# A fused attention and expert kernel: the first step's four gate and up pieces are also stored split, and loaded finished seven steps later

## What is computed

```python
gate = jnp.einsum('btd,edf->ebtf', x, Wg)
up = jnp.einsum('btd,edf->ebtf', x, Wu)
gate = gate.at[:NL].add(jnp.einsum('btd,edr,erf->ebtf', x, Ga, Gb))
up = up.at[:NL].add(jnp.einsum('btd,edr,erf->ebtf', x, Ua, Ub))
mid = jax.nn.silu(gate) * up
out = jnp.einsum('ebtf,efd->ebtd', mid, Wd)
out = out.at[:NL].add(jnp.einsum('ebtf,efr,erd->ebtd', mid[:NL], Da, Db))
return jnp.einsum('bte,ebtd->btd', weights, out)
```

## Time and profile before

| | us |
|---|---|
| median of 3 runs | 1043.31 |
| lowest, highest | 1042.74, 1044.19 |
| the profiled execution's own time | 1044.28 |
| its span in the profile | 1042.5 |
| busy: PE, PEld | 1029.0, 841.7 |
| busy: DVE, ACT, POOL | 751.0, 457.8, 80.3 |
| granted clock of TensorE, mean | 1.00 |
| 24 pairs of stores to piece_spill, by POOL | 896 KB each |
| bytes moved in all | 173.43 MB |

### The profile page before, as it was taken

How to read it: one execution, slowest core, us unless ns; L and a number is a source line. 1 busy time by engine, 2 the same in 40 slices (tenths; PEclk the granted TensorE clock), 3 DMA queues, 4 the chain that set the end, 5 groups by cost and what they waited for, 6 DMA issues and landing times.

```text
span 1042.5 us, 12575 instructions
## 1 busy us (share of the span) xinstructions
PE 1029.0 (99%) x4641; PEld 841.7 (81%) x4641; DVE 751.0 (72%) x1268; ACT 457.8 (44%) x708; POOL 80.3 (8%) x113
## 2 busy tenths in 40 slices
PE   7999999999999999999999999999999999999998
PEld 5887877878888888888888788888888888888886
DVE  6878678967484765758566695886868586977664
ACT  4664363563353343425434344453635263534530
POOL 2511121100001000000100011000000000000000
PEclk9999999999999999999999999999999999999999
DMA  9410104249557483855748674525343544444342
GB/s 297 161 51 1 81 21 162 76 112 297 201 194 269 141 275 132 281 194 196 265 132 289 206 254 120 183 96 219 118 172 103 212 131 165 159 162 162 106 177 81
DMA packets 95709, 173.43 MB, mean 166 GB/s; under 512 B 5728, under 2 KB 62240, under 8 KB 94752
## 3 DMA queue, kind: packets, MB, share of 16 engines
q1 hardware_dynamic: 87584, 125.37, 36.8%
q0 software_dynamic: 7776, 47.19, 12.2%
q10 hardware_dynamic: 288, 0.07, 0.0%
HBM read 111.23 MB, written 61.37 MB: 166 GB/s over the span
## 4 chain that ended last, share of the span: by engine, by line
PE 83%; DVE 9%; DMA 2%; ACT 2%; issue 2%; SPq 0%; POOL 0%; DVEq 0%
PE gate_up L2045 15%; PE gate_up L2047 15%; PE gate_up L2046 15%; PE tiles L1931 6%; PE tiles L1933 6%; PE tiles L1932 6%; PE tiles L2065 4%; PE tiles L2064 4%; PE tiles L2063 4%; PE gate_up L2002 2%; PE gate_up L2003 2%; PE gate_up L2008 2%; DVE piece_lo L1422 1%; PE tiles L1967 1%; DMA wd_raw<-in_wd_dram 1%
## 5 line engine op out<-in xcount | busy, mean ns | idle before, releaser
L2045 PE MATMUL gate_up<-xT_hi,piece_hi 128*128 128x512 f32 x448 | 175.0, 391 | 0.5 <-DVE mids L1463 0.3
L2047 PE MATMUL gate_up<-xT_lo,piece_hi 128*128 128x512 f32 x448 | 174.4, 389 | 0.0
L2046 PE MATMUL gate_up<-xT_hi,piece_lo 128*128 128x512 f32 x448 | 174.3, 389 | 0.0
L2045 PE MATMUL gate_up<-tx_hi,piece_hi 128*128 128x512 f32 x336 | 131.1, 390 | 1.6 <-DVE gates L1451 1.6
L2046 PE MATMUL gate_up<-tx_hi,piece_lo 128*128 128x512 f32 x336 | 130.8, 389 | 0.0
L2047 PE MATMUL gate_up<-tx_lo,piece_hi 128*128 128x512 f32 x336 | 130.8, 389 | 0.0
L1422 DVE TENSOR_TENSOR piece_lo<-piece,piece_hi 128x1024 fp32r<-128x1024 f32 x88 | 93.1, 1099 | 29.0 <-ACT piece_hi L956 28.4
L969 ACT ACTIVATE gate_up<-gate_up 128x512 f32<-128x512 f32 x56 | 32.6, 582 | 182.7 <-PE gate_up L2047 122.1
L1931 PE MATMUL tiles<-wd_hi,mids_hi 128*128 128x512 f32 x256 | 99.7, 390 | 0.4 <-DVE mids_lo L1504 0.4
L2045 PEld LDWEIGHTS gate_up<-xT_hi,piece_hi 128*128 128x128 f32 x448 | 84.1, 188 | 19.5 <-issue 0.7
L1933 PE MATMUL tiles<-wd_hi,mids_lo 128*128 128x512 f32 x256 | 99.6, 389 | 0.0
(11 more groups left out here) (214 smaller groups left out, 1914.9 us busy)
## 6 DMA issues: line engine op xcount, KB each, us to landing
piece_spill<-piece_hi POOLq DMA_DIRECT2D x24, 896.0 KB, 4.6
piece_spill<-piece_lo POOLq DMA_DIRECT2D x24, 896.0 KB, 6.8
piece_hi<-piece_spill SPq DMA_DIRECT2D x24, 896.0 KB, 4.5
piece_lo<-piece_spill SPq DMA_DIRECT2D x24, 896.0 KB, 6.4
piece<-in_wg_dram SPq DMA_DIRECT2D x24, 256.0 KB, 4.3
piece<-in_wu_dram SPq DMA_DIRECT2D x24, 256.0 KB, 6.2
merged<-lora_w SPq DMA_DIRECT2D x6, 1024.0 KB, 6.1
wd_raw<-in_wd_dram SPq DMA_DIRECT2D x5, 1024.0 KB, 5.3
```

What stands on the lines that cost most here:

```text
L2045: nc.tensor.matmul(dst, w_h, x_h, start=first and kt == 0, stop=False, skip_group_check=True)
L2046: nc.tensor.matmul(dst, w_l, x_h, start=False, stop=False, skip_group_check=True)
L2047: ins = nc.tensor.matmul(dst, w_h, x_l, start=False, stop=last and kt == 1, skip_group_check=True)
```

## The change

Two constants change. Pieces 0 to 3 are stored too, and the pieces of step 7 count as finished. The functions that read these constants do the rest.

```diff
-FINISHED = [which != DOWN and SWAP < k for k, which, m in QUADS]
-FIRST_STORED, LAST_STORED = 4, 4 * SWAP
+FINISHED = [which != DOWN and SWAP <= k for k, which, m in QUADS]
+FIRST_STORED, LAST_STORED = 0, 4 * SWAP
```

## The result

The changed kernel takes **1047.93 us** (median of 4 runs, 1047.43 to 1049.25) against 1043.42 us for the kernel before (4 runs beside it, 1042.74 to 1044.19). The ratio is 1.0045, with a 95% interval from 1.0033 to 1.0057: slower by 0.45%; the medians are 4.5 us apart. The profiled execution took 1047.81 us and its span is 1046.0 us, against 1044.28 and 1042.5: 3.5 us more in both.

A forecast was written before the change was run, and what follows sets the result against it. PE, busy 99% of the span, was taken to bound the kernel, with wd_raw's chain without slack. +4.1 (wd_raw) + 0.4 (piece 3) - 0.6 (piece 28) = +3.9 us on the median 1043.31 gave 1047.2, range 1043.4 to 1050.8.

The forecast's parts named there:

- What bounds the kernel: Whole kernel: PE is busy 99% of the span; wd_raw's chain in step 0 has no slack, so its delay is PE's.
- wd_raw +4.1: Step 0: behind the stores of pieces 0 and 1, wd_raw lands at 218.5 instead of 214.43, costing PE 4.1 us.
- the order of arrival: DMA queues in step 0: transfers issued earlier are served first; forecast 1045.4 to 1048.6, chance 0.50.
- turns: Rival, step 0: queues share engines packet by packet, wd_raw gets 2/9 of bytes; about +6.5, 1048.6 to 1051.4, chance 0.21.
- store 2 arrives at 214: Step of the packet-sharing rival, step 0: piece 2's store reaches the engines at 214 and is served beside the remaining loads.
- The price of each pair: Step 0: each pair of stores occupies all 16 DMA engines for 4.6 us, starting 1.2 us after its issue.
- Piece 3, +0.4: Step 0: piece 3's load, issued at 216.6 instead of 212.53, makes PE wait 0 to 1.1 us more; taken as +0.4.
- Piece 28, -0.6: Before step 7: without piece 28's sums and split, PE's stall at 618.97 goes, worth 0.56 us, taken as -0.6.
- Step 7's larger loads, 0: Step 7: four loads grow from 512 KB to 1792 KB, landing 6.4 us after second issue; PE waits for none, price 0.
- The stall of step 6, 0: Step 6: the 1.05 us stall at 581.34 hangs on pieces 25 to 27, made as before, so no change.

The follow-up runs named there:

- the loads alone: Kernel before, with step 7's pieces loaded finished from the places of pieces 4 to 7, pieces 0 to 3 not stored: 1042.73 us, ratio 0.9996.
- the stores alone: Changed kernel's stores of pieces 0 to 3 kept, step 7's pieces loaded raw and made as before: 1049.72 us, ratio 1.0063 against the kernel before.
- both reorders: Changed kernel with wd_raw's load ahead of acc_spill and piece 3's load ahead of the wait for acc_spill and the LoRA factors: 1043.27 us, ratio 0.9997.
- the kernel with 12.55 us of idle time: Changed kernel with piece 0 stored twice, the second time to a spare place, so three pairs of stores stand ahead: 1056.19 us, ratio 1.0119.

## Why the prediction was right, and where it was not

**What bounds the kernel** was read rightly. wd_raw's chain had no slack, and its delay of 3.8 us at the landing came out of PE whole (+4.17, with the 0.4 by which the kernel started earlier).

**wd_raw +4.1: the number held, its reason did not.** I had it from the order of arrival, for which I took the 354 packets against 28 of the earlier trace rows. That row is a window of 1 us in which q0 had only just started. In the windows 253 to 253.5 and 254 to 254.5 the kernel before shows

```profile
q1 hardware_dynamic: 243, 0.12, 98.7%
q0 software_dynamic: 8, 0.06, 35.4%
...
q0 software_dynamic: 27, 0.19, 92.9%
q1 hardware_dynamic: 36, 0.02, 11.5%
```

so q1 was nearly alone at first and the two were near equal turns at the end. The rival "turns" had the mechanism, as the run with piece 0 stored twice shows. That it did not give its +6.5 here is a matter of two microseconds. Stores and acc_spill have rows of about the same size, so turns or no turns they are through together. Store 2 was issued at 212.64, but its first packets come after 215; the queues in the changed kernel in the windows 209-210, 213-214 and 215-216:

```profile
q1 hardware_dynamic: 28, 0.23, 55.9%
q0 software_dynamic: 26, 0.18, 44.1%
...
q1 hardware_dynamic: 170, 0.32, 88.5%
q0 software_dynamic: 3, 0.01, 3.5%
...
q1 hardware_dynamic: 152, 0.28, 79.8%
q0 software_dynamic: 19, 0.14, 32.3%
```

With the 185 packets between 214 and 215, wd_raw had 170 + 185 + 152 = 507 of its 512 packets of 2 KB moved or moving by 216. With one more pair ahead it met stores from its start nearly to its end, first piece 1's and then store 2, and took 7.9 us longer. The step of the rival that failed is "store 2 arrives at 214".

**The price of each pair** (4.6 us of all engines, less the head start) is right for the sum of two, and wrong one by one. Piece 0's pair alone costs nothing, piece 1's alone 3.2 us at wd_raw, both together 4.1 (all from landings after the issue). I had put 1.9 on the pair of piece 1 alone. 0.8 of the miss is the start of SP's transfers, 0.7 us and not 1.2 after an issue that came 0.3 earlier; the rest is open. The same correction leaves the sum for both pairs near what it was, since POOL began 0.6 us earlier too: through at 199.43 + 1.2 + 9.2 = 209.8, acc_spill's start at 204.72 + 0.7 = 205.4, so 4.4 us, which is what acc_spill lost.

**Piece 3, +0.4: measured about 0.** Its load was issued at 218.95 and not at 216.6, since SP's own issues of the LoRA factors took 1.4 us each and not 0.6. But its chain stood behind ACT's copy of the third quad's product, which PE sets; piece 3 and PE came to the fourth quad together. As soon as wd_raw was out of the way this term came up at 2.1 us. It was small here because a larger stall ahead covered it.

**What was missing: the clock, +1.3.** The prediction says nothing of what a long idle time of PE does to the work behind it. PE's idle times of 3.77, 3.83, 4.72, 5.59 and 12.55 us in five of these kernels were each followed or ended by a granted clock of 0.50; those of 3.00 and 1.65 us in two others were not.

**Piece 28, -0.6: held, at -0.7.** No wait is left at the mids before step 7 in the changed kernel, with the loads alone, or with piece 28 alone loaded finished; it is there (0.45) with only piece 29 loaded finished and (0.46) with the stores alone.

**Step 7's larger loads, 0: held**, with landings of up to 10.9 us in place of 6.4 (the low part of piece 29 in the changed kernel).

**The stall of step 6, 0: it measured -0.7, unexplained.** It took 0.31 to 0.63 us in six of the seven kernels that store all four pairs, but 1.02 in the seventh (both reorders); in the seven that store one, a half or none, it took 0.80 to 1.41. So it may go with the stores, through a way that I have not found, since between 250 and 581 us all these kernels issue the same transfers. It stays open.

So +4.1 + 0.4 - 0.6 = +3.9 was forecast. On the profiled execution it came as +4.2 + 0 + 1.3 - 0.7 = +4.8, less 0.4 at the start of the kernel, 0.7 in step 6 and 0.1 to 0.2 in the rest: +3.5. The medians are +4.5 apart; one profiled execution of each kernel can't tell which part is larger there. That the total came out so near is in part luck: the clock that was missing (+1.3) and the parts that came out lower (-0.4 of piece 3, -0.4 at the start, -0.7 in step 6) have opposite signs, and for two pairs of these stores the order of arrival gives the same delay as the turns that the queues took.

## What to carry to other kernels

Before a window of two queues is read as a rule of who goes first, cut it finer, until both queues have work waiting from its first moment to its last; then compare the packets, and price a transfer with short rows by its share of the bytes.
A store that nothing waits for is not free if a load on the matrix engine's path is issued behind it before it is through: here a pair issued 5.3 us before SP's next transfer cost nothing, one issued 2.4 us before it cost wd_raw 3.2 us. Ask also what else of short rows stands behind it, for moving the store or the load each time moved a part of the loss to the next transfer.
If a change makes the matrix engine idle for several microseconds at a stretch, add to the sum the matmuls behind it at half speed (here after 3.77 us and more, not after 3.00).

## What the runs showed of the hardware

- **A stop of PE costs more than itself.** The clock was back at 1.00 some 2.8 us after PE went on in the changed kernel, and 5.7 us after it in the kernel with 12.55 us of idle time. The end of those 5.7 us in PE's order of time (0.43 us to the next start, then 0.30):

```profile
236.75 0.63 PE L2049 MATMUL gate_up<-xT_hi,piece_hi 128*128 128x512 f32 x1
237.18 0.46 PE L2050 MATMUL gate_up<-xT_hi,piece_lo 128*128 128x512 f32 x1
237.48 0.40 PE L2051 MATMUL gate_up<-xT_lo,piece_hi 128*128 128x512 f32 x1
```

- **A queue joins late.** acc_spill's first packets came 0.4 to 0.9 us after its issue with idle engines, but 3.8 to 4.4 us after it with two or three pairs of stores in flight (208.5 to 209 in the changed kernel, after 204.72; 209 to 209.5 with three, after 205.12), and from then on the queues took turns, however much was left in the other (10 packets against 22 in its first half microsecond with three pairs, 23 against 27 a microsecond later). Until it joined, q0 had the engines alone. Why it joins when it does, no run here tells.
- **Issuing took longer with stores in flight.** SP's issue of wd_raw took 0.44 us before, 1.20 in the changed kernel, 1.58 with three pairs ahead; those of the LoRA factors 0.60 and up to 1.43, or 1.64 with three pairs.
